# VectorE rounds the first tile of an FP4 input group in its old slot and the other three tiles one slot later, GpSimd's passes with them

## What is computed

```python
def fp4_quant_dequant(x):               # blocks of 16 along the last dim
    scale = jnp.max(jnp.abs(xb), axis=-1, keepdims=True) / 6.0
    scale = jnp.maximum(scale, jnp.float32(1e-12))
    xn = xb / scale
    idx = jnp.searchsorted(_MID, jnp.abs(xn))
    q = _GRID[idx] * jnp.sign(xn) * scale
...
gate = fp4_linear(x, w_gate); y = fp4_linear(x, w_up)
h = jax.nn.silu(gate) * y
return fp4_linear(h, w_down)            # h is quantised too
...
x = x + ga * _L0_attn_ref(h, ...)       # layer 0, attention
h = _layernorm(x) * (1 + cb) + sb
x = x + gb * _L0_ffn_ref(h, ...)        # layer 0, FP4 feed-forward
...                                     # layer 1: attention, then a mixture of experts
```

## Time and profile before

| what | value |
|---|---|
| median of 3 runs | 701.55 us (701.0 to 701.91) |
| the profiled execution's own time | 702.42 us |
| its span, first to last instruction | 699.5 us |
| PE busy | 632.3 us, 90% |
| PE weight loads busy | 484.7 us, 69% |
| DVE busy | 473.2 us, 68% |
| ACT busy | 343.6 us, 49% |
| POOL busy | 249.6 us, 36% |
| mean granted TensorE clock | 0.990 |

### The profile page before, as it was taken

How to read it: one execution, slowest core, us unless ns; L and a number is a source line. 1 busy time by engine, 2 the same in 40 slices (tenths; PEclk the granted TensorE clock), 3 DMA queues, 4 the chain that set the end, 5 groups by cost and what they waited for, 6 DMA issues and landing times.

```text
span 699.5 us, 11088 instructions
## 1 busy us (share of the span) xinstructions
PE 632.3 (90%) x3839; PEld 484.7 (69%) x3839; DVE 473.2 (68%) x1262; ACT 343.6 (49%) x709; POOL 249.6 (36%) x328
## 2 busy tenths in 40 slices
PE   5889899998788999998899999878899997998996
PEld 4456687877566777775678777756778874676774
DVE  5966589786797447626569886598544537766665
ACT  1133464565546464533445565464555545454553
POOL 3424756463764221004557465486310002000000
PEclk9999999999999999999999999999999999999999
DMA  8200000000000000000000000110000000001011
GB/s 270 66 1 1 2 1 1 1 1 1 1 1 0 3 1 0 1 2 1 1 0 1 1 1 1 29 30 1 0 1 1 1 1 1 1 15 31 15 31 30
DMA packets 12173, 9.64 MB, mean 14 GB/s; under 512 B 1804, under 2 KB 10840, under 8 KB 12120
## 3 DMA queue, kind: packets, MB, share of 16 engines
q1 hardware_dynamic: 12120, 8.95, 4.3%
HBM read 6.84 MB, written 2.10 MB: 13 GB/s over the span
## 4 chain that ended last, share of the span: by engine, by line
PE 64%; DVE 17%; ACT 9%; issue 5%; POOL 3%; DMA 1%; SPq 0%; ACTq 0%; POOLq 0%; DVEq 0%
PE ps L849 14%; PE ps L714 11%; PE ps L827 8%; PE ps L673 4%; PE ps L999 4%; PE ps L1001 4%; PE ps L1000 4%; PE ps L872 2%; ACT xn L1117 2%; PE ps L873 2%; PE ps L888 2%; POOL rstd L518 2%; PE ps L668 2%; DVE row_max L1451 1%; DVE xn L1333 1%
## 5 line engine op out<-in xcount | busy, mean ns | idle before, releaser
L1182 ACT ACTIVATE probsT<-ps 128x512 f32<-128x512 f32 (+3 forms) x160 | 85.4, 534 | 162.3 <-PE ps L827 162.3
L849 PE MATMUL ps<-v_sb,probsT 128*128 128x129 f32 (+1 forms) x1124 | 151.4, 279 | 3.7 <-ACT probsT L1184 3.7
L849 PEld LDWEIGHTS ps<-v_sb,probsT 128*128 128x128 f32 (+1 forms) x1124 | 137.6, 191 | 8.8 <-ACT probsT L1184 5.5
L1451 DVE TENSOR_REDUCE row_max<-ps 128x1 f32<-128x512 f32 (+2 forms) x144 | 87.5, 619 | 54.3 <-PE ps L722 27.8
L827 PE MATMUL ps<-ident,probs 128*128 128x128 f32 (+1 forms) x562 | 90.1, 276 | 15.8 <-ACT hT L1109 7.8
L1156 ACT ACTIVATE probs<-ps,neg_max 128x512 f32<-128x512 f32 (+7 forms) x158 | 93.0, 620 | 9.0 <-DVE neg_max L1458 6.8
L827 PEld LDWEIGHTS ps<-ident,probs 128*128 128x128 f32 (+1 forms) x562 | 63.3, 139 | 47.8 <-issue 43.9
L554 POOL TENSOR_TENSOR hq<-ha,hp 128x352 f32<-128x352 f32 x32 | 29.9, 933 | 98.0 <-DVE hp L1501 98.0
L668 PE MATMUL ps<-unpick,ident_b 128*128 128x512 bf16 x196 | 47.8, 386 | 1.1 <-ACT v_sb L1248 1.1
L714 PE MATMUL ps<-k_high,q_high 128*128 128x512 f32 (+5 forms) x100 | 42.1, 421 | 4.8 <-ACT probs L1156 4.8
L1263 ACT ACTIVATE probs<-ps 128x512 f32<-128x512 f32 x40 | 24.0, 599 | 44.0 <-PE ps L1001 44.0
(11 more groups left out here) (246 smaller groups left out, 1404.1 us busy)
## 6 DMA issues: line engine op xcount, KB each, us to landing
out<-x_sb SPq DMA_DIRECT2D x8, 256.0 KB, 2.3
x_sb<-in_L_attn_x SPq DMA_DIRECT2D x2, 512.0 KB, 5.5
hT_all<-in_L_wmod SPq DMA_DIRECT2D x2, 384.0 KB
rope_cos<-table_cos SPq DMA_DIRECT2D x1, 768.0 KB, 6.1
rope_sin<-table_sin SPq DMA_DIRECT2D x1, 768.0 KB, 8.8
rope_cos<-table_cos SPq DMA_DIRECT2D x1, 256.0 KB, 3.6
rope_sin<-table_sin SPq DMA_DIRECT2D x1, 256.0 KB, 5.4
moe_raw<-in_L_ffn_expert_gate_w SPq DMA_DIRECT2D x1, 256.0 KB, 2.7
```

The lines of the kernel that those rows point to most:

```text
L849: mm = pe.matmul(bank(OUT_AT, 0, V_W), probsT[0:size, n % 4, k * P:(k + 1) * P], v_sb[0:size, j, :], start=(c == 0 and k == 0), stop=(c == ...
L1182: ins = act.activation(probsT[:, n % 4, 0:full], bank(TURN, 0, full), ACT.Copy)
L1451: ins = dve.tensor_reduce(dst, ps[:, start:start + width], AX.X, ALU.max, negate=single)
```

## The change

`fp4_input` and `xq_scaled` take a part. Part 0 (one tile, 128 columns) stands where the whole stood, at the end of slots 4, 8, 12, 16. Part 1 (three tiles, 384 columns) stands in the next slot: on VectorE between `quantise_h` and `finish`, on GpSimd at the slot's end. Part 0 waits only for its own tile's `h_shifted`. The work on GpSimd is the same six passes for each group.

```diff
-                def xq_scaled(g):
-                    pool.wait_ge(xq_grid, b * GROUPS + g + 1)
+                def xq_scaled(g, part):
+                    a, z = FP4_PARTS[part]
+                    pool.wait_ge(xq_grid, 2 * (b * GROUPS + g) + part + 1)
                     if g >= 1:
                         pool.wait_ge(turned, TURN_AT[b, "fp4_rest", g - 1] + 1)
-                    for part, (a, z) in enumerate(FP4_PARTS):
...
                     if at(FP4_SLOT) is not None:
-                        xq_scaled(at(FP4_SLOT))
+                        xq_scaled(at(FP4_SLOT), 0)
+                    if at(FP4_SLOT + 1) is not None:
+                        xq_scaled(at(FP4_SLOT + 1), 1)
...
-                def fp4_input(g):
+                def fp4_input(g, part):
+                    a, z = FP4_PARTS[part]
+                    cols, scales = slice(a * P, z * P), slice(a * P // BLOCK, z * P // BLOCK)
+
                     def scales_used():
                         if g:
                             dve.wait_ge(xq_ready, 2 * (b * GROUPS + g))
 
-                    dve.wait_ge(h_shifted, b * TILES + (g + 1) * GROUP)
-                    quantise(qa[:], qp[:], xn[:, g, :], GROUP * P // BLOCK, qs, scales_used).then_inc(xq_grid, 1)
+                    dve.wait_ge(h_shifted, b * TILES + g * GROUP + z)
+                    quantise(qa[:, cols], qp[:, cols], xn[:, g, cols], (z - a) * P // BLOCK, qs[:, :, scales],
+                             scales_used).then_inc(xq_grid, 1)
...
                     if ffn_tile(s, FFN_LAG) is not None:
                         quantise_h(s - FFN_LAG)
+                    if group_at(s, FP4_SLOT + 1) is not None:
+                        fp4_input(group_at(s, FP4_SLOT + 1), 1)
...
                     finish(s)
                     if group_at(s, FP4_SLOT) is not None:
-                        fp4_input(group_at(s, FP4_SLOT))
+                        fp4_input(group_at(s, FP4_SLOT), 0)
```

More of the change, by code:

```diff
@@ L560, in hq_scaled @@
                         [P, INNER // BLOCK, BLOCK]), ALU.mult).then_inc(hq_ready, 1)
-                def xq_scaled(g):
-                    pool.wait_ge(xq_grid, b * GROUPS + g + 1)
+                def xq_scaled(g, part):
+                    a, z = FP4_PARTS[part]
+                    pool.wait_ge(xq_grid, 2 * (b * GROUPS + g) + part + 1)
                     if g >= 1:
                         pool.wait_ge(turned, TURN_AT[b, "fp4_rest", g - 1] + 1)
-                    for part, (a, z) in enumerate(FP4_PARTS):
[L567 to L575, removed]
+                    cols, done = slice(a * P, z * P), b * 4 * GROUPS + 4 * g + 2 * part
+                    pool.tensor_tensor(xq[:, cols], qa[:, cols], qp[:, cols], ALU.add).then_inc(xq_step, 1)
+                    pool.wait_ge(xq_step, done + 1)
+                    pool.tensor_tensor(xq[:, cols], xq[:, cols], qp[:, cols], ALU.subtract).then_inc(xq_step, 1)
+                    pool.wait_ge(xq_step, done + 2)
+                    by_block = xq[:, cols].rearrange("p (k e) -> p k e", e=BLOCK)
+                    scales = qs[:, 2, a * P // BLOCK:z * P // BLOCK].unsqueeze(2)
+                    pool.tensor_tensor(by_block, by_block, scales.to_broadcast([P, (z - a) * P // BLOCK, BLOCK]),
+                                       ALU.mult).then_inc(xq_ready, 1)
                 def rope_sum(g, which):
```

## The result

The changed kernel takes 707.09 us (median of 4 runs, 707.04 to 709.66) against 701.73 for the kernel before beside it: a ratio of 1.0082, 95% interval 1.0065 to 1.01. It is slower by 0.8%, some 5.4 us; the forecast was 4.6. Three of its four executions, the profiled one among them, have a mean granted clock of 0.990 and took 707.04, 707.05 and 707.13; the fourth, at 0.983, took 709.66. The profiled execution has a span of 705.2 us against 699.5. That the total is right is partly luck, as the places show.

The account below looks back on a forecast made before the run. TensorE's list sets most of the time, but VectorE's carries the path in groups 1 and 3. 2 x (0.9 + 1.4) = 4.6 us on 701.55 gives 706.1, the forecast's own range 704.0 to 708.2, overall 700.9 to 708.9.

Parts of the forecast that it names:

- Price of the pass, and the turns of VectorE and GpSimd: VectorE's split pass: 4.0 us clean instead of 2.94, 1.06 more a group, plus waits for GpSimd's passes on a shared port.
- the third rival: TensorE's clock falls too in group 3, behind new idle time: about 1 us a batch more, 708.1; chance 17%.
- the second: Rival without waits between VectorE and GpSimd at the new widths: only 1.06 us a group added, 701.3; chance 16%.
- The 1.53 for 128 columns: Part 0 on VectorE: clean price of 1.53 us for a pass over 128 columns.
- Group 1, +0.9: Slots 9 to 11: a gain of 0.7 us from part 0, then part 1 takes 3.7; net 0.9 later a batch.
- over 1 was named as a sign: Sign in slot 11's exp: ScalarE waits over 1 us for the negated maximum.
- Group 2, zero: Part 1 in slot 13 delays VectorE by up to 3.7 us, covered by its 2.08 wait and the exp's 0.8 spare.
- 8.5 to 14: Sign on VectorE over the eight groups: busy time rises by 8.5 us clean, up to 14 with waits.
- Group 3, +1.4: Part 1 takes 4.65 us beside GpSimd, `q1_low` ends later, TensorE starts at 208.2 instead of 206.82: 1.4 a batch.
- half of a busy stretch of that length, 1.7, partly hidden: Price of a clock fall in group 3, from group 0's 3.41 us at 0.51 speed: about 1 us a batch.
- Group 0, zero: Part 1 in slot 5 delays VectorE by up to 3.7 us, inside its 2.90 wait at 86.94; no net change.
- Sum: Both batches of groups 1 and 3 together: 2 x (0.9 + 1.4) = 4.6 us, giving 706.1.

Follow-up runs that it names:

- only group 3 split: Against the kernel before, only group 3's pass is split, the other groups doing all 512 columns in their old slot: 707.47 us, ratio 1.0079.
- changed, part 1 first: The changed kernel with part 1 ahead of `quantise_h` in VectorE's list, GpSimd's order the same: 709.67 us, ratio 1.0101 to the kernel before.
- before + filler in 0: The kernel before with four matmuls of no use at the start of slot 5: 701.53 us, ratio 0.9986.
- 0 and 2 split + filler in 0: Against the kernel before, groups 0 and 2 split and four matmuls of no use at the start of slot 5: 698.13 us, ratio 0.994.
- Changed + both fillers: The changed kernel with four useless matmuls at the start of slot 5 and six ahead of slot 18's down product: 702.56 us, ratio 1.0008.

## Why the prediction was right, and where only its sum was

- *Price of the pass, and the turns of VectorE and GpSimd.* Right: 2.48 clean for 384 columns (forecast 2.47), 3.79 in group 1 (3.7), 4.71 in group 3 (4.65). The rule of the Trainium skill's "SBUF — State Buffer" (Who interferes with whom) holds at the new widths: at 384 columns the scaling took 1.03 beside GpSimd and 0.56 without it, the exponent 0.83 and 0.36, and the block maximum 0.55 and 0.54. The forecast's own sentence names the third rival for the case without these waits; it is the second. The 1.53 for 128 columns never appears clean: in groups 0, 1 and 3 that pass shared its time with GpSimd and took 2.1, 3.2 and 2.7.
- *Group 1, +0.9.* Right: +0.91 to +0.95 in eight places. TensorE's gap ahead of the scores of tile 10 is gone and comes back as 1.08 ahead of the down product and 0.72 of ScalarE's waiting, where over 1 was named as a sign.
- *Group 2, zero.* Right, though part 1 took 4.73 there and not 3.7 at most: `finish(13)` is 4.7 late, and `finish(14)` is on time again. This and part 1's 3.3 in group 0 are part of why VectorE is busy 17.9 us longer and not 8.5 to 14.
- *Group 3, +1.4.* Right as far as it went: +1.24 with the clock held. But the third rival came true on top of it. It had 17% and 1 us a batch; the clock fell in all six places where group 3 was split without a filler, and 6.83 us ran at the lower level in five of them, not 3.41: in the changed kernel and in only group 3 split that cost 1.8 to 2.1 a batch, and the one fall of 3.41 cost 0.9. The mis-sized term was "half of a busy stretch of that length, 1.7, partly hidden", and the chance was too low for a place where the clock fell six times of six, four times behind a gap of 1.91 or 1.92 and twice within the 3.7 us of "changed, part 1 first". That the gap was longer than the known one of 1.61 would not have settled it, as the gap of 2.06 below shows.
- *Group 0, zero.* Wrong. The failed sentence is "Group 0: TensorE has no gap that VectorE's pass causes". It was true of the one profile read, and only because TensorE was at 1.2 GHz there. With its clock up the kernel before waits 1.22 us at that place, and the split wins 1.5 to 1.7. I used that low clock as a price for group 3, and did not ask what it hid where it stood.
- *Sum.* In the profiled execution the two errors, +1.7 to 1.9 and -1.7 a batch, nearly cancel. The forecast's 706.1 was right by its terms for groups 1 and 2, and by this cancelling for the rest. Its range of 2.1 either way is not worked out from the 0.9 allowed for each net, which would be 3.6 if all four erred one way. Of other executions there are only times and mean clocks; they do not say in which place the clock fell.

What stays open: what decides whether the clock falls behind the gap of 1.61 in group 0. It fell in 8 of 18 places without a filler there and in none of 8 with one; the split did not decide it (3 of 8 places with it, 5 of 10 without). The length of the gap does not decide it alone either. Behind the second batch, at 583 to 592 us and in code that no kernel here changes, TensorE waits 2.06 or 2.07 us in every profile, and behind it the clock fell in 5 of 13. The same 32 matmuls, first in "before + filler in 0", with the clock at 0.5, then in "0 and 2 split + filler in 0", with it up:

```profile
588.26 3.55 PE L971 MATMUL ps<-ident_b,xn 128*128 128x128 bf16 x32 [2.07 <-DVE xn L1616]
```
```profile
584.89 1.96 PE L983 MATMUL ps<-ident_b,xn 128*128 128x128 bf16 x32 [2.06 <-DVE xn L1634]
```

## What to carry to other kernels

Before a place is called free of an engine's influence, look at the granted clock there: where TensorE runs at half speed, waits for other engines can vanish from its rows, as the 1.22 us did here, and an edit that shortens them may show nothing until the clock is held. Put a step that two engines take turns on where the other is idle, not directly behind the instruction that starts the other; here that was 1.3 of 3.8 us. But follow what the new order pushes back: the same exchange gained 0.7 a batch in group 1 and lost 1.6 in group 3. When an edit opens a gap of TensorE near 2 us, count the lower clock behind it as a real chance (here four places of four in group 3, and 5 of 13 at another gap of that length), and try a few matmuls of no use in the gap.

## What was not expected of the hardware

- After the 1.91 us gap in group 3 the clock stayed at 0.5 for 6.83 us, twice the 3.41 of group 0. In only group 3 split, a gap of 1.91 or 1.92 gave 6.83 in one batch and 3.41 in the other.
- Half speed for 3.41 us in group 0 cost the kernel before only 0.2 us, and 1.7 once that group was split; in group 3 it cost 0.9, and 6.83 us cost 1.8 to 2.1. What it costs hangs on what else waits there, not on the length alone.
- With four or six short matmuls in a gap the clock stayed up in all 12 places where they stood. No cost shows: the kernel before with the filler gains the same 0.2 a batch as in its second profile, without a filler and without the low clock, and in slot 18 TensorE still waits 0.63 us behind the filler. "Changed + both fillers" has no low clock ahead of its last microseconds, which is partly chance, for the gap of 2.06 has no filler.
